# Scatter stage of a four-layer GNN kernel: a third region of edge tiles, its sums in and behind the last pairs, and no ones beside early sums

## What is computed

```python
row, col = (edge_index[0], edge_index[1])                     # src, dst (dst is sorted)
edge_aggr = jnp.zeros((x.shape[0], edge_attr.shape[1]), dtype=x.dtype)
edge_aggr = edge_aggr.at[row].add(edge_attr).at[col].add(edge_attr)
node_features = jnp.concatenate([x, edge_aggr], axis=1)
h = jax.nn.relu(node_features @ W1 + b1)
return h @ W2 + b2
```

## Time and profile before

| | us |
|---|---|
| median of 3 runs (lowest, highest) | 1226.16 (1221.59, 1229.09) |
| the profiled execution | 1231.04 |
| its span, first to last instruction | 1229.2 |
| PE busy over the span | 1099.2 (89%) |
| DVE busy | 894.9 (73%) |
| POOL busy | 705.3 (57%) |
| ACT busy | 628.0 (51%) |
| mean granted TensorE clock | 0.952 |

### The profile page before, as it was taken

The page is one execution under the profiler, slowest core; times in us unless marked ns, Lnnn a source line. Parts: engine busy times, 40 slices in busy tenths (PEclk is TensorE's granted clock), DMA queues, the critical chain, the costliest instruction groups (busy, mean ns, idle before and its releaser), DMA issues. The chain is left out here.

```text
span 1229.2 us, 31958 instructions
## 1 busy us (share of the span) xinstructions
PE 1099.2 (89%) x9519; PEld 933.5 (76%) x9520; DVE 894.9 (73%) x3140; ACT 628.0 (51%) x1794; POOL 705.3 (57%) x720
## 2 busy tenths in 40 slices
PE   6999885999999999925987899989899999999996
PEld 3666553888787888824854799974799999999985
DVE  6998875678777889886777754456577777777763
ACT  8665544888988888866632311023233333333322
POOL 4777777777777777781000000007777777777772
PEclk9998999999999999977998899987999999999998
DMA  7675334565555566545851000027878888888861
GB/s 237 182 209 158 105 106 114 165 165 151 162 152 154 179 199 186 162 136 153 247 11 55 2 2 2 1 64 210 236 216 220 221 222 236 223 214 230 236 165 52
DMA packets 177186, 188.62 MB, mean 153 GB/s; under 512 B 44319, under 2 KB 136844, under 8 KB 176876
## 3 DMA queue, kind: packets, MB, share of 16 engines
q1 hardware_dynamic: 142086, 136.92, 42.2%
q0 software_dynamic: 22656, 46.87, 12.7%
q10 hardware_dynamic: 12264, 2.70, 1.1%
HBM read 140.19 MB, written 44.28 MB: 150 GB/s over the span
## 5 line engine op out<-in xcount | busy, mean ns | idle before, releaser
L2610 POOL DMA_INDIRECT between<-p_table,src_g x292 | 287.7, 985 | 361.8 <-DMA p_table<-n_nm 273.0
L981 POOL DMA_INDIRECT rows_by_block<-h_t,mean_bc x312 | 311.6, 999 | 106.2 <-issue 84.9
L471 PE MATMUL acc<-ones_b 128*128 128x128 bf16 (+1 forms) x925 | 157.9, 296 | 49.5 <-PEq L911 33.0
L1112 DVE TENSOR_TENSOR between<-between,acc 128x600 f32 x208 | 161.5, 776 | 51.9 <-PE acc L1266 41.1
L1255 PE MATMUL acc<-n_nm 128*128 128x384 bf16 (+1 forms) x832 | 142.5, 294 | 38.2 <-issue 27.5
L2751 ACT ACTIVATE between<-acc 128x128 f32<-128x128 f32 x138 | 38.3, 278 | 225.3 <-PE acc L2868 197.4
L1076 DVE TENSOR_SCALAR n_nm<-iota_w,agg_sum 128x600 bf16<-128x600 f16 x416 | 143.1, 386 | 0.0
L1000 ACT ACTIVATE away<-iota_b,agg_sum 128x128 bf16<-128x128 bf16 x416 | 140.9, 385 | 0.0
L1255 PEld LDWEIGHTS acc<-n_nm 128*128 128x128 bf16 x832 | 72.3, 98 | 86.0 <-issue 35.1
L471 PEld LDWEIGHTS acc<-ones_b 128*128 128x128 bf16 x925 | 72.4, 100 | 76.6 <-issue 60.5
L2851 PE MATMUL acc<-weights,between 128*128 128x128 f32 x584 | 128.4, 302 | 0.0
(11 more groups left out here) (296 smaller groups left out, 2557.3 us busy)
## 6 DMA issues: line engine op xcount, KB each, us to landing
h_t<-in_edge_rows SPq DMA_DIRECT2D x78, 260.0 KB, 3.1
between<-in_edge_columns SPq DMA_DIRECT2D x36, 512.0 KB
between<-in_dst SPq DMA_DIRECT2D x36, 288.0 KB
held<-rows_by_block SPq DMA_DIRECT2D x69, 130.0 KB
h_t<-rows_by_block SPq DMA_DIRECT2D x34, 260.0 KB, 3.7
by_dst<-q_whole_table SPq DMA_DIRECT2D x138, 64.0 KB
x_nm<-rows_by_block SPq DMA_DIRECT2D x30, 260.0 KB
agg_sum<-in_edge_rows SPq DMA_DIRECT2D x26, 260.0 KB
```

The lines of the kernel that those rows point to most:

```text
L471: pe.matmul(acc[:, bank * BANK + skip:(bank + 1) * BANK].rearrange("p (a n) -> p a n", n=P), ones_b[:, :], ones_b[:, :].rearrange("p (a n) ...
L981: pool.indirect_dma_start(rows_by_block, bass.IndirectOffsetOnAxis(ap=place_in_table[:, t:t + 1], axis=0), row_group(g)[:, j, :], None).th ...
L1112: dve.tensor_tensor(between[:, :, bass.ds(first, W)], between[:, :, bass.ds(first, W)], acc[:, o:o + NB * WS].rearrange("p (b w) -> p b w" ...
L2610: pool.indirect_dma_start(got[:, q, j * D:(j + 1) * D], None, p_table, bass.IndirectOffsetOnAxis(ap=src_g[:, n * G + j:n * G + j + 1], axi ...
```

## The change

Tiles 252 to 355 become a region of their own, between the second one, which now ends at tile 251, and the late one, which begins at tile 356. The new region has 129 tiles of room, the late one 77 in place of 181, read in 25 reads. The new region has 25 reads, one for each block: twelve on pairs 184 to 206, and thirteen on steps 208 to 220 behind the last pair, for which the loops of SP, PE, ACT and DVE go on for 18 steps (`AFTER_PAIRS`). Hots of reads behind pair 204 are all made by DVE. Wide reads now lie on pairs 70 to 130, those of the second region on 134 to 182. PE's ones stop at the first early sum. x is loaded a first time at group 26, and its statistics and averages are taken in pairs 48 to 65; the final load stays where it was. ACT checks seven counts at the end of the scatter stage and six in the late stage; the other twelve are joined by DVE, one in each step behind the pairs. The addition of `held` to the sums by destination moves from the late stage to the end of the scatter stage. Small checks (`oddities`) move there too.

```diff
-TILES_MID = 256
+TILES_MID = 252
 GROUPS_MID = TILES_MID // KC
+TILES_MID2 = 356
+GROUPS_MID2 = TILES_MID2 // KC
...
+def cap_mid2(b):
+    return 6 if 15 <= b < 21 else 5 if b < NB - 1 else 3
...
 def cap1(b):
-    return 7 if b < 15 else 8 if b < NB - 1 else 4
+    return 3 if b < 21 else 4 if b < NB - 1 else 2
...
-CHECKED_AT_END, CHECKED_BY_ACT = 5, 18
+CHECKED_AT_END, CHECKED_BY_ACT = 7, 13
...
-            TAILS = 7
+            TAILS = 11
             READS_AFTER = 4
+            MID2_IN_PAIRS = 12
+            AFTER_PAIRS = NB - MID2_IN_PAIRS + TAKE_AFTER
+            X_LOAD_AT, X_ZERO_AT, X_STATS_AT = 26, 36, 48
...
-            read_pairs = {(78 + r * 68 // wide_reads if r < wide_reads else 148 + (r - wide_reads) * 52 // NB): r for r in range(len(early_reads))}
+            def pair_of_read(r):
+                if r < wide_reads:
+                    return 70 + r * 62 // wide_reads
+                if r < wide_reads + NB:
+                    return 134 + (r - wide_reads) * 50 // NB
+                n = r - wide_reads - NB
+                return 184 + 2 * n if n < MID2_IN_PAIRS else PAIRS + n - MID2_IN_PAIRS
...
             def by_dve(r):
-                return r % 3 == 2
+                return r % 3 == 2 or pair_of_read(r) > PAIRS - SUM_AFTER
...
                         if r == 0:
-                            sp.wait_ge(tail_zero.h, tail_zero.at(16 * TAILS))
+                            sp.wait_ge(x_stats.h, x_stats.at(2))
...
+                        if g == X_LOAD_AT:
+                            sp.wait_ge(vec.h, vec.at(1))
+                            sp.dma_start(x_nm[:, 0:NB - 1, :], x[0:(NB - 1) * P, :].rearrange("(b p) f -> p b f", p=P)).then_inc(x_in.h, 16)
...
-                    for i in range((GROUPS - READS_AFTER) * PG, PAIRS):
+                    for i in range((GROUPS - READS_AFTER) * PG, PAIRS + AFTER_PAIRS):
                         if i in read_pairs:
                             early_read(read_pairs[i])
-                    sp.wait_ge(vec.h, vec.at(1))
                     sp.wait_ge(nodes_summed.h, nodes_summed.at(len(early_reads)))
                     sp.wait_ge(kept.h, kept.at(wide_reads))
                     sp.dma_start(x_nm[:, 0:NB - 1, :], x[0:(NB - 1) * P, :].rearrange("(b p) f -> p b f", p=P)).then_inc(loaded.h, 16)
...
-                    for i in range(PAIRS + 2):
+                    for i in range(PAIRS + AFTER_PAIRS):
...
+                        x_statistics(i)
+                        if i == PAIRS + AFTER_PAIRS - 2:
+                            oddities()
+                        if PAIRS + 2 <= i < PAIRS + 2 + NB - CHECKED_BY_ACT:
+                            join_counts(i - PAIRS - 2)
...
-                    dve.wait_ge(loaded.h, loaded.at(16 * 23))
-                    for b in range(NB):
-                        dve.bn_stats(stats[:, b, :], x_nm[:, b, :])
+                    dve.wait_ge(agg_read.h, agg_read.at(NSB + 2 * NB))
+                    dve.tensor_tensor(held[:, :], held[:, :], agg_dst[:, 0:NSB * SBN], ALU.add)
...
-                        if not first_sum <= i < after_sums:
+                        if i < first_sum:
                             stream_ones(pe, IDLE_BANK, warm)
...
-                        if first_sum <= i < after_sums:
-                            stream_ones(pe, at_bank(i) // BANK + 1, warm + 1, 3 * P)
```

More of the change, by code:

```diff
@@ L314, in build @@
         bases = sb("bases", [1, 2, NK])
-        over = Space(n_flat[:, 2944:NP], F32).take([1, 6, NB])
+        over = Space(n_flat[:, 2944:NP], F32).take([1, 8, NB])
         rel2 = sb("rel2", [P, TILES_HERE])
@@ L361, in build @@
         bounds_space = Space(mean_bc[:, 2500:NP], F32)
[L362 to L363 removed]
+        base_rows = bounds_space.take([1, 4, NK])
+        past_step = pair_far[0:1, 0:4 * NK].rearrange("p (k n) -> p k n", k=4)
         ends2 = bounds_space.take([1, NK])
         ends_mid = bounds_space.take([1, NK])
[L366 removed]
+        ends_mid2 = bounds_space.take([1, NK])
+        bounds = bounds_space.take([1, 8, NB])
         keys_space = Space(mean_bc[:, 2500:NP], F32)
@@ L767, in build @@
         checked = signal("checked")
+        x_in, x_stats = tabs_in, idx_read
+        late = signal("late")
         early_away = of_block = signal("of_block")
@@ L844, in early_reads_by_source @@
                 reads.append((NSB + b, base_mid(b), cap_mid(b), True, True))
+            for b in range(NB):
+                reads.append((NSB + NB + b, base_mid2(b), cap_mid2(b), True, True))
             return reads
@@ L886, in place_and_count @@
             last_early = {read[0]: r for r, read in enumerate(early_reads)}
-            read_pairs = {(78 + r * 68 // wide_reads if r < wide_reads else 148 + (r - wide_reads) * 52 // NB): r for r in range(len(early_reads))}
+            def pair_of_read(r):
[5 more added lines that the diff above has]
+                return 184 + 2 * n if n < MID2_IN_PAIRS else PAIRS + n - MID2_IN_PAIRS
+            assert AFTER_PAIRS >= 2 + NB - CHECKED_BY_ACT
+            read_pairs = {pair_of_read(r): r for r in range(len(early_reads))}
+            assert max(read_pairs) + TAKE_AFTER < PAIRS + AFTER_PAIRS and len(set(read_pairs)) == len(early_reads)
             assert len(read_pairs) == len(early_reads)
@@ L1038, in _ @@
                     base_of_next(0)
-                    for i in range(PAIRS):
-                        lows(i)
+                    for i in range(PAIRS + AFTER_PAIRS):
+                        if i < PAIRS:
+                            lows(i)
                         r = early_of_pair(i - TAKE_AFTER)
@@ L1284, in place_and_count @@
                 s.passed(made_by_act(len(early_reads)))
-            agg_read.passed(NSB + NB)
+            agg_read.passed(NSB + 2 * NB)
+            late.passed(5)
+            x_in.passed(32)
+            x_stats.passed(2)
             checked.passed(CHECKED_AT_END)
@@ L1405, in build @@
         upd_made = signal("upd_made")
-        late = signal("late")
         keys_made = signal("keys_made")
```

190 lines of the change are left out of this document (115 added, 75 removed).

## The result

The changed kernel takes 1273.76 us (median of 4 runs, 1268.10 to 1278.15) against 1227.38 us: a ratio of 1.0357, 95% interval 1.0325 to 1.0389, slower by 3.6%. The sign was forecast, the size was not: 46 us in place of 20, and outside the range of 1228 to 1264.

| us from the span's start | before | after | forecast |
|---|---|---|---|
| DVE's last collection ends | 532.96 | 544.06 | 537.5 |
| POOL's last scatter ends | 559.74 | 557.15 | 555 to 570 |
| PE's last early sum ends | 520.71 | 603.74 | 587.5 |
| late stage starts | 564.37 | 628.04 | 610.5 |
| next stage's first instruction | 622.74 | 659.65 | 642.9 |

A forecast was written before the change was run, and what follows sets the result against it. The prediction took POOL's scatters to bound the scatter stage, with a long late stage behind. Late stage starting 46.1 us later, less 26.0 gained in it, gave +20.1 on 1226.2: 1246 us, range 1228 to 1264.

The forecast's parts named there:

- Late stage: Stage behind the scatter stage: 77 late tiles for 181 and 25 reads for 50, 32.4 us against 58.4, gaining 26.0.
- End of the pairs: Scatter stage: sums run on through pair 207, so DVE's last collection ends 4.5 us later, at 537.5.
- upper bound of 540: End of the pairs at the latest, if nothing is given back for the time PE saves.
- Thirteen reads: Behind the pairs: DVE and PE form a chain of 3.85 us a step, 50 us, last early sum done at 587.5.
- rival (3): Behind the pairs: sums run at half clock, step 5.1 us, 16 us more, 1262; chance 0.17.
- The reads: Behind the pairs: three buffers and 4.2 us landing make two steps take 7.9 us, 3.95 each.
- SP's load: Between last early sum and late stage: final load of x and weights is uncovered, 23.0 us, late stage starts at 610.5.
- Early edits: Before and in the pairs: extra zeroing, early x load and statistics, about 7 us of DVE, covered and costing nothing.
- rival (4): Scatter stage: the early load starves POOL, its end moves by up to 10 us; pairs 10 us later give 1256; chance 0.06.
- Rival (1): Behind the pairs: no chain, DVE's own 2.35 us sets the pace, 19.5 us less, 1227; chance 0.11.
- Rival (2): In the pairs: without ones PE runs ahead, pairs end at 521, 16.5 us less, 1230; chance 0.11.
- signs listed for "wrong": SP's x load before 570, late stage within 5 us of POOL's end or over 40 us, pairs ending before 525 or after 545.

The follow-up runs named there:

- e1: Changed kernel with PE again running four small matmuls of ones in each pair from the first early sum on: 1269.71 us, ratio 1.0338.
- e2: Changed kernel with eight large matmuls of ones on PE behind each early sum from step 211 on: 1258.63 us, ratio 1.0222.
- e10: The changed kernel run once more, nothing altered: 1272.53 us, ratio 1.0350.
- e3: Changed kernel with DVE adding each block ahead of the next hots and join, from step 211 on: 1241.98 us, ratio 1.0091.
- e9: e6 with the 21 loads of weights issued by ACT behind the last early sum: 1224.57 us, ratio 0.9950.
- e6: Changed kernel with the addition first as in e3, and ones in the pairs and behind each sum from step 211: 1238.71 us, ratio 1.0055.
- e7: e6 with the weights issued by SP two at a time between the late stage's reads: 1232.89 us, ratio 1.0039.

## Why the prediction was wrong

- *Late stage: right, part by part.* 32.4 forecast, 31.6 measured: ones 3.9, sums 23.7 for the 23.5 forecast, closing work 4.0.
- *End of the pairs: too early by 6.6 us (537.5 against 544.06).* The step that failed is "PE loses its ones (0.23 us a pair there)": they were counted as load alone, and what PE does without them, stand still and fall to 1.2 GHz, was given no price in the pairs. With them DVE's last collection ends at 538.57 (e1). The upper bound of 540, "with nothing given back", does not follow from the rows either: 2.26 x 7 - 10.9 = 4.9 gives 537.9, and the measured end lies beyond both.
- *Thirteen reads: the chain was right, its sum mis-sized.* "Add 0.28, six hots 1.37, a sum of 1.35, a join 0.92" is what stands in the step, and at full clock e2 has 50.3 us for the 50 forecast. The term that failed is the sum of ten matmuls at 1.35 us: in eight steps it took 2.48, or 2.90 with twelve, and the thirteen steps 9.7 us more in all. That was rival (3), held at 0.17 and priced at 16 us more. Its mechanism happened, and its price was too high, since not every sum ran at the lower level (12.8 us with 12 of 15 in e10). The Trainium skill (TensorE: Matmul & The Clock Gate, HAM oscillation — how this bites in real kernels) tells of bursts shorter than the waits behind them, each of which starts at half clock. The trace agrees in part: 8 of 15 sums ran wholly at half clock, not each, and none once ones fill the waits (e2). I had the row that spoke for it and left it undecided.
- *The reads: a wrong argument beside a right number.* "Two steps take 7.9" would hold the step at 3.95 whatever DVE's order. e3 has steps of 2.3 us with the same three buffers. The chain alone gives 3.7 x 13 = 48.1 us, so the agreement of 50 with e2's 50.3 owes 1.9 us to this argument, and that part is luck.
- *SP's load: right.* 23.0 forecast, 24.3 measured; from the last issue to the six reads it took 5.1 us in place of 3.1. It was on the path by its issues, and ACT could have taken them (e9).
- *Early edits: nothing, right.* POOL ended at 557.15, ahead of the 559.74 before; rival (4) fell. No run took these edits out alone. Rival (1) fell as the kernel stands, and e3 shows which order would have made it true. Rival (2) fell: without ones PE did not run ahead, in either kernel.
- *Sum.* The forecast of +20.1 missed 6.6 (pairs) + 9.7 (sums) + 1.3 (load) - 0.8 (late stage) = 16.8 us up to the end of the late stage, and 10.2 behind it, for which it had no term. The range ended at 1264 because it held the lower clock as one rival's price behind the pairs, and nothing for it in the pairs. None of the signs listed for "wrong" came: they asked whether there was a chain, and what failed was the length of its steps, mostly 4.0 to 5.5 us in place of 3.5 to 4.2.

## What to carry to other kernels

Matmuls of ones on an engine that waits were not load to be saved here: before taking them out, price every wait that they cover at the lower clock, by the same instruction's rows at both levels. Where one engine works for another step by step, look in its order for what stands between "the result is there" and "the next may start": moving one addition ahead of two other instructions was worth 17 us here at full clock, and 25 where the clock had been falling. And a load that was hidden is paid in full once its cover is gone (24.3 us here); with the weights on an idle engine's queue, the 24.1 us of e6 came down to 11.9 (e9).

## What the runs showed of the hardware that I had not expected

Between sums of 1.6 us with waits of 2.4 to 2.6 us the granted clock fell, and not at every step: 2.90 us for the sum at 566.01, 1.59 for the same twelve matmuls at 581.51. The clock at one place differs between executions of one program (1.81 and 1.00 us for the same eight matmuls in the second layer), 5.6 us over that stretch. Twenty-one small loads cost about 10 us of a stage when SP issued them between its reads; when ACT, idle, issued them just ahead of it, they cost 1.4 in the stage (33.1 us against e6's 31.7) and 2.0 before it (11.9 us from the last sum against 9.9 in e7).
